# Second mixture of experts on chosen rows only: rows scattered into expert slots, 23 tiles of 512 slots, results scattered and added at the end

## The reference

```python
scores = softmax(xf @ Wg.T)                       # xf: 4096 rows of 128, normalised
expert_weights, expert_indices = top_k(scores, 2)
expert_weights = expert_weights / expert_weights.sum(-1)
gates = (one_hot(expert_indices, 8) * expert_weights[..., None]).sum(axis=1)
g = silu(lora_in(xf, W1, b1, A1, B1)) * lora_in(xf, W3, b3, A3, B3)   # all 8 experts, 256 wide
y_e = lora_out(g, W2, b2, A2, B2)
y = einsum('te,ted->td', gates, y_e)              # six of the eight gates of a row are zero
```

## Time and profile before

| what | value |
|---|---|
| median of 3 executions | 1125.36 us (1123.95 to 1134.6) |
| the profiled execution | 1127.59 us |
| its span, first to last instruction | 1126.4 us |
| TensorE, VectorE, ScalarE, GpSimd busy | 77%, 69%, 40%, 38% |
| second MoE in it | 799.2 to 1126.4 us |

### The profile page before, as it was taken

How to read it: one execution, slowest core, us unless ns; L and a number is a source line. 1 busy time by engine, 2 the same in 40 slices (tenths; PEclk the granted TensorE clock), 3 DMA queues, 4 the chain that set the end, 5 groups by cost and what they waited for, 6 DMA issues and landing times. The chain is left out here.

```text
span 1126.4 us, 20278 instructions
## 1 busy us (share of the span) xinstructions
PE 872.6 (77%) x6496; PEld 644.1 (57%) x6496; DVE 773.8 (69%) x3299; ACT 451.6 (40%) x1123; POOL 426.2 (38%) x767
## 2 busy tenths in 40 slices
PE   0976766765577998537891388988699999999998
PEld 0753433432374554424561256666488888888887
DVE  7949999999334886371130869999567666766664
ACT  1454445444103555101132657877333333333332
POOL 5213666666545542016663655655200100010000
PEclk9975666667557999767996569999799999999999
DMA  8211111111103000005533100000000000000000
GB/s 171 64 40 31 36 36 35 37 36 31 30 13 150 19 23 24 10 6 100 84 107 121 45 2 3 3 3 3 1 1 10 11 1 11 10 10 1 10 10 10
DMA packets 66078, 37.98 MB, mean 34 GB/s; under 512 B 39482, under 2 KB 60083, under 8 KB 65460
## 3 DMA queue, kind: packets, MB, share of 16 engines
q1 hardware_dynamic: 63206, 32.31, 10.5%
q0 software_dynamic: 2048, 4.20, 2.5%
q10 hardware_dynamic: 718, 0.17, 0.1%
HBM read 26.11 MB, written 10.55 MB: 33 GB/s over the span
## 5 line engine op out<-in xcount | busy, mean ns | idle before, releaser
L1759 ACT ACTIVATE e_sg<-e_ps,vec 128x512 f32<-128x512 f32 x128 | 88.1, 689 | 182.7 <-PE e_ps L1720 182.0
L1680 PEld LDWEIGHTS e_psy<-w_folded,e_hh 128*128 128x128 f32 x1024 | 124.1, 192 | 5.2
L1680 PE MATMUL e_psy<-w_folded,e_hh 128*128 128x128 f32 x1024 | 124.5, 275 | 0.0
L1858 DVE SCALAR_TENSOR_TENSOR e_hh<-e_ps,vec,e_sg 128x512 f32<-128x512 f32 x128 | 94.6, 748 | 42.5 <-ACT e_sg L1759 39.7
L1846 DVE SCALAR_TENSOR_TENSOR X<-e_psy,e_gs,X 128x128 f32<-128x128 f32 x256 | 72.1, 344 | 56.5 <-PE e_psy L1680 56.5
L1718 PE MATMUL e_ps<-e_XH,e_wh 128*128 128x512 f32 x256 | 110.0, 430 | 0.0
L1720 PE MATMUL e_ps<-e_XH,e_wl 128*128 128x512 f32 x256 | 101.7, 397 | 0.0
L1719 PE MATMUL e_ps<-e_XL,e_wh 128*128 128x512 f32 x256 | 101.4, 396 | 0.0
L1448 POOL TENSOR_SCALAR a_kb<-a_kr,a_m,a_bk 128x128 f32<-128x128 f32 x128 | 57.9, 452 | 51.8 <-issue 36.8
L758 DVE MATCH_REPLACE8 work<-m,work 128x64 f32<-128x64 f32 x384 | 75.8, 208 | 0.0
L745 DVE MAX8 m<-work 128x8 f32<-128x64 f32 x384 | 57.1, 210 | 0.0
(11 more groups left out here) (367 smaller groups left out, 2135.8 us busy)
## 6 DMA issues: line engine op xcount, KB each, us to landing
toe<-s4d_kernel SPq DMA_DIRECT2D x64, 64.0 KB
planes<-rt_zeros SPq DMA_DIRECT2D x4, 1024.0 KB, 6.9
ew<-in_L_ffn_ew SPq DMA_DIRECT2D x16, 256.0 KB
comb_y<-planes SPq DMA_DIRECT2D x16, 256.0 KB, 5.7
X<-in_x SPq DMA_DIRECT2D x4, 512.0 KB, 6.8
fold_wr<-in_L_ffn_W SPq DMA_DIRECT2D x16, 128.0 KB, 2.3
rows<-XT SPq DMA_DIRECT2D x8, 256.0 KB, 2.0
out_dram<-X SPq DMA_DIRECT2D x8, 256.0 KB, 2.3
```

What stands on the lines that cost most here:

```text
L1680: mm = pe.matmul(psy[j][:, k, :], hh[j][:, c, k * P:(k + 1) * P], G.w2[:, e, c, :], start=(c == 0 and k == 0), stop=(c == NC - 1), skip_gr ...
L1759: act.activation(sg[j][:, c, :], psh[0][c][:], ACT.Silu, bias=G.vec[:, k:k + 1]).then_inc(silu[c], 1)
L1858: dve.scalar_tensor_tensor(hh[j][:, c, :], psh[1][c][:], G.vec[:, k:k + 1], sg[j][:, c, :], ALU.add, ALU.mult).then_inc(hh_sb[c], 1)
```

## The change

`second_experts` is split in three phases, and two earlier phases prepare for it.

- `first_experts`: VectorE no longer makes `e_wh` and `e_wl`. SyncE's late DMAs get four more, which store the folded weights and biases of the eight experts in DRAM (`folded_weights`, 395 KB for each expert).
- `second_attention`: SyncE fills a DRAM table `expert_slots` with vacant rows by 79 DMAs of 128 x 2080 bytes (21 MB). A row of it has 130 words: 128 values, the number of the row's home, its gate.
- `second_router` (new): blocks b of 512 rows as before. VectorE picks the two experts of each row and computes each choice's slot from a running count; GpSimd stores the rows, 128 with each indirect DMA, 8 for each block. At the end VectorE writes a table of 23 tiles: which expert, and which first slot. 23 tiles of 512 slots suffice for any choice (8192 / 512 + 7). The biases of the output layer are added here.
- `second_experts` (new): a loop over the 23 tiles i. SyncE reads the tile's entry from the table, and loads its rows (`xr`, 4 buffers) and its expert's weights (`wf`, 3 buffers). TensorE turns the rows of tile i + 1, computes the hidden products of tile i and the output product of tile i - 1. The splitting into high and low parts is now done for each tile, for rows and weights. VectorE scales the results by the gate (`ys`, 3 buffers), and GpSimd scatters them to DRAM (`expert_pairs`) with 4 indirect DMAs for each tile.
- `combine_pairs` (new): both results of each row are loaded, VectorE adds them to `G.X`, and the output is stored.

The core of the diff (the old function is printed above):

```diff
+STILE = 512
+NTILE = 2 * B * T // STILE + NE - 1
+SROWS = (NE - 1) * B * T + NTILE * STILE
+SPARE = 2 * B * T
+ROW = D + 2
...
+                n13, n2 = 2 * HE, HE // P * D
+                kept = G.folded.rearrange("e p w -> p e w")
+                later += [(kept[:, :, 0:n13], G.w13[:].rearrange("d e m c p -> d e (m c p)")),
+                          (kept[:, :, n13:n13 + n2], G.w2[:].rearrange("p e c d -> p e (c d)"))]
+                for m, n in enumerate("13"):
+                    v = VEC["L1_ffn_b" + n][0]
+                    later += [(kept[:, :, n13 + n2 + 2 * m:n13 + n2 + 2 * m + 2], G.vec[:, v:v + 2 * NE].rearrange("p (e c) -> p e c", e=NE))]
...
-                    dve.tensor_copy(G.wh[:, e, :, :, :], G.w13[:, e, :, :, :]).then_inc(s["high"], 1)
-                    dve.wait_ge(s["high"], e + 1)
-                    dve.tensor_tensor(G.wl[:, e, :, :, :], G.w13[:, e, :, :, :], G.wh[:, e, :, :, :].bitcast(F32), ALU.subtract).then_inc(s["low"], 1)
...
+            @block.sync
+            def _(sp):
+                sp.wait_ge(s["vacant"], 1)
+                slots = G.slots.rearrange("(i p k) w -> p i k w", p=P, k=STILE // P)
+                n = SROWS // STILE
+                for i in range(n):
+                    sp.dma_start(slots[:, i, :, :], vacant[:]).then_inc(s["cleared"], 16)
+                sp.wait_ge(s["cleared"], n * 16)
...
+                dve.memset(vacant[:], 0.0).then_inc(s["spare"], 1)
+                dve.wait_ge(s["spare"], 2)
+                dve.tensor_copy(vacant[:, :, D:D + 1].bitcast(U32).rearrange("p k a -> p (k a)"), vacant_i[:]).then_inc(s["vacant"], 1)
...
-def second_experts(nc, C, A, G):
...
+def second_router(nc, C, A, G):
...
+                for b in range(NBLK):
+                    if b + 2 < NBLK:
+                        root(b + 2)
+                    pool.wait_ge(s["slot"], b + 1)
+                    pool.wait_ge(s["twice"], b + 1)
+                    for k in range(2):
+                        for t in range(TB):
+                            pool.indirect_dma_start(G.slots, bass.IndirectOffsetOnAxis(ap=slot[:, b, k, t:t + 1], axis=0),
+                                                    rb[b % NB][:, k, t, :], None).then_inc(sent[b % NB], 16)
+                for j in range(NB):
+                    pool.wait_ge(sent[j], 2 * TB * 16 * len(range(j, NBLK, NB)))
...
+                    after(dve, sent[b % NB], 2 * TB * 16 * (b // NB))
+                    normalise_block(dve, rb[b % NB][:, 0, :, 0:D], G.X[:, tiles(b), :], part(b)).then_inc(s["xs"], 1)
...
+                def choose(b):
+                    w = part(b)
+                    dve.wait_ge(s["logits"], b + 1)
+                    dve.tensor_copy(w["lg"], psl[:, 0:TB * NE].rearrange("p (k e) -> p k e", e=NE)).then_inc(s["lg"], 1)
+                    dve.wait_ge(s["lg"], b + 1)
+                    largest(b, 0)
+                    step.then(dve.scalar_tensor_tensor(w["lg"], oh[:, b, 0, :, :], TAKEN, w["lg"], ALU.mult, ALU.add))
+                    largest(b, 1)
+                    TT(w["d"], w["m1"], w["m0"], ALU.subtract).then_inc(s["d"], 1)
+                    step.then(TT(w["sel"], oh[:, b, 0, :, :], oh[:, b, 1, :, :], ALU.add))
+                    for t in range(b * TB, (b + 1) * TB):
+                        m = TT(run[:, t + 1, :], run[:, t, :], full["sel"][:, t, :], ALU.add)
+                        if t + 1 < (b + 1) * TB:
+                            step.then(m)
+                    m.then_inc(s["sel"], 1)
...
+                def place(b):
+                    w = part(b)
+                    dve.wait_ge(s["ranks"], b + 1)
+                    step.then(TT(w["pos"], psr[:, 0:TB * NE].rearrange("p (k e) -> p k e", e=NE), wide(first[:].unsqueeze(1), shape), ALU.add))
+                    step.then(TT(prod[:, b], oh[:, b], wide(w["pos"].unsqueeze(1), [P, 2, TB, NE]), ALU.mult))
+                    step.then(dve.tensor_reduce(slotf[:, b], prod[:, b], AX.X, ALU.add))
+                    dve.tensor_copy(slot[:, b], slotf[:, b]).then_inc(s["slot"], 1)
...
+                for b in range(NBLK):
+                    if b + 2 < NBLK:
+                        statistics(b + 2)
+                    choose(b)
+                    if b + 1 < NBLK:
+                        normalise(b + 1)
+                    gates(b)
+                    place(b)
+                    if b > 0:
+                        add_biases(b - 1)
+                table()
+def second_experts(nc, C, A, G):
...
+            @block.sync
+            def _(sp):
+                for i in range(NTILE):
+                    e = sp.value_load(G.tiles[0:1, 0, i:i + 1], min_val=0, max_val=NE - 1)
+                    row = sp.value_load(G.tiles[0:1, 1, i:i + 1], min_val=0, max_val=SROWS - STILE)
+                    if i >= NX:
+                        sp.wait_ge(kept[(i - NX) % NY], ((i - NX) // NY + 1) * S * 16)
+                    sp.dma_start(xr[i % NX][:], G.slots[bass.ds(row, STILE), :].rearrange("(p k) w -> p k w", k=S)).then_inc(rows[i % NX], 16)
+                    after(sp, s["y"], i - NW + 1)
+                    after(sp, hh_sb[NC - 1], i - NW + 1)
+                    sp.dma_start(wf[i % NW][:], G.folded[bass.ds(e, 1), :, :].rearrange("a p w -> p (a w)")).then_inc(weights[i % NW], 16)
+            @block.tensor
+            def _(pe):
+                def turn(i):
+                    pe.wait_ge(rows[i % NX], (i // NX + 1) * 16)
+                    after(pe, s["x_low"], i - 1)
+                    for k in range(S):
+                        mm = pe.transpose(pst[i % 2][:, k * P:(k + 1) * P], xr[i % NX][:, k, 0:D], G.ident[:])
+                    mm.then_inc(s["turned"], 1)
+                def product(i):
+                    j = i % 2
+                    after(pe, s["y_sb"], i - 1)
+                    for c in range(NC):
+                        pe.wait_ge(hh_sb[c], i + 1)
+                        for k in range(S):
+                            mm = pe.matmul(psy[j][:, k, :], hh[j][:, c, k * P:(k + 1) * P], wf[i % NW][:, 2 * HE + c * D:2 * HE + (c + 1) * D],
+                                           start=(c == 0 and k == 0), stop=(c == NC - 1), skip_group_check=True)
+                    mm.then_inc(s["y"], 1)
+                turn(0)
+                for i in range(NTILE):
+                    j = i % 2
+                    if i + 1 < NTILE:
+                        turn(i + 1)
+                    pe.wait_ge(s["x_low"], i + 1)
+                    pe.wait_ge(s["w_low"], i + 1)
+                    for c in range(NC):
+                        for m in range(2):
+                            after(pe, hh_sb[c], i)
+                            pe.matmul(psh[m][c][:], wh[j][:, m, c, :], XH[j][:], start=True, stop=False)
+                            pe.matmul(psh[m][c][:], wh[j][:, m, c, :], XL[j][:], start=False, stop=False)
+                            pe.matmul(psh[m][c][:], wl[j][:, m, c, :], XH[j][:], start=False, stop=True).then_inc(h_ps[m][c], 1)
+                    if i > 0:
+                        product(i - 1)
+                product(NTILE - 1)
+            @block.scalar
+            def _(act):
+                act.preload_act_table(ACT.Silu)
+                def high(i):
+                    act.wait_ge(weights[i % NW], (i // NW + 1) * 16)
+                    after(act, h_ps[1][NC - 1], i - 1)
+                    act.activation(wh[i % 2][:], w13(i), ACT.Copy).then_inc(s["w_high"], 1)
+                    act.wait_ge(s["turned"], i + 1)
+                    act.activation(XH[i % 2][:], pst[i % 2][:], ACT.Copy).then_inc(s["x_high"], 1)
+                high(0)
+                for i in range(NTILE):
+                    if i + 1 < NTILE:
+                        high(i + 1)
+                    for c in range(NC):
+                        k = 2 * HE + NC * D + c
+                        act.wait_ge(h_ps[0][c], i + 1)
+                        after(act, hh_sb[c], i - 1)
+                        act.activation(sg[i % 2][:, c, :], psh[0][c][:], ACT.Silu, bias=wf[i % NW][:, k:k + 1]).then_inc(silu[c], 1)
+            @block.gpsimd
+            def _(pool):
+                for i in range(NTILE):
+                    pool.wait_ge(s["y_sb"], i + 1)
+                    for k in range(S):
+                        pool.indirect_dma_start(G.pair, bass.IndirectOffsetOnAxis(ap=home[i % NY][:, k:k + 1], axis=0),
+                                                ys[i % NY][:, k, :], None).then_inc(kept[i % NY], 16)
+                for j in range(NY):
+                    pool.wait_ge(kept[j], S * 16 * len(range(j, NTILE, NY)))
+            @block.vector
+            def _(dve):
+                def low(i):
+                    dve.wait_ge(s["w_high"], i + 1)
+                    after(dve, h_ps[1][NC - 1], i - 1)
+                    dve.tensor_tensor(wl[i % 2][:], w13(i), wh[i % 2][:].bitcast(F32), ALU.subtract).then_inc(s["w_low"], 1)
+                    dve.wait_ge(s["x_high"], i + 1)
```

(70 more changed lines are left out.)

340 lines of the change are left out of this document (152 added, 188 removed).

## The result

The changed kernel takes 1159.06 us (median, 1155.36 to 1167.64), the kernel before 1125.09 on the same chip: a ratio of 1.0294 (95% interval 1.0214 to 1.0373). The profiled execution is the longest of them, 1167.64 us with a span of 1166.4. Of its excess 7.4 us lie in phases that the change leaves as they are: the phase that makes the first router's slots ends at 509.3 us here and at 501.9 in the trace of before. Some executions of most kernels are 7 to 14 us longer than their others, so where two versions are near each other I compare the phases in their traces.

A forecast was written before the change was run, and what follows sets the result against it. The prediction took TensorE alone to set the pace of the old second MoE. Start 799.2 + router 116 + tile loop 221.5 + adding the pairs 22 = 1158.7 us of span; forecast 1158 us, range 1132 to 1202.

The forecast's parts named there:

- Ahead of the phase, 0: Before the second MoE: vacant-row stores and folded weights cost 0 us, with ends of -3 and +5.
- The router, 116: Router phase: GpSimd's stores set it, one indirect DMA each 1.28 us; with start, inverse roots, landing and drain 116 us.
- VectorE is hidden: Router: VectorE needs 9.6 us for a block, less than GpSimd's 12, so it does not show.
- The weighed rule on VectorE shutting out GpSimd: Router: VectorE's float32 scalings keep GpSimd from writing descriptors, 9 us by the rule; left out of the sum.
- The tile loop, 221.5: Loop over 23 tiles: waiting for landed results sets the pace; with fill, last steps and drain 221.5 us.
- L: Tile loop: path from the end of an output product through scaling, stores and landing to the next rows, 11.1 us.
- T: Tile loop: length of a step, 9.0 us, half of a pair of 18.0 us; ends 8.05 and 11.5.
- the round trip does not bind: Rival, tile loop: GpSimd's stores set the pace, a step of 5.1 us, 1084 us in all; chance 0.06.
- The clock, 1.9 us a pair: Tile loop: after each pause TensorE starts at the lower level of 1.2 GHz, adding 1.9 us to a pair of steps.
- the clock stays low: Rival, tile loop: the clock stays at 1.2 GHz throughout, a step of 10.5 us, 1186 us in all; chance 0.17.
- The end of the loop: After the last product: GpSimd's remaining stores, landing, then a drain from 214.6 to 219.9 us, SyncE's first load at 221.5.
- the drains are shorter by half: Part of a rival: the clock holds (a step of 8.05 us) and both drains halve, 1134 us; chance 0.13.

The follow-up runs named there:

- the version with half the stores: Changed kernel with GpSimd storing only the first choices' rows in the router, 32 stores instead of 64; not a version to keep: 1138.72 us, ratio 1.0171.
- the three versions at 6.5: Changed kernel with rows loaded once VectorE has scaled tile i - 4 (0.9885); with five row buffers (0.9913); with that load rule plus four weight buffers (0.993).
- earlier release: Changed kernel, but SyncE loads the rows of tile i once VectorE has scaled tile i - 4, not once its results have landed: 1116.57 us, ratio 0.9885.
- work in the pause: Changed kernel with 22 matmuls on the identity, whose result nobody reads, ahead of every second tile's transposes: 1149.3 us, ratio 1.0201.

## Why the prediction was right

Against the profiled execution the four terms were:

| term | forecast | measured |
|---|---|---|
| start of the second MoE | 799.2 | 806.2 |
| router, to the first load of rows | 116 | 113.6 |
| tile loop, to the first load of results | 221.5 | 224.0 |
| adding the pairs, to the end | 22 | 22.5 |

The router came out 2.4 us shorter and the loop 2.5 us longer; that these cancel is luck, but either is small beside the 34 us of the slowdown.

*Ahead of the phase, 0.* This was right for the stores of vacant rows, which are all issued and waited for by 721.6 us, 84 us before the attention ends. The phase that stores the folded weights takes 106.3 us (509.4 to 615.7), before 106.1. The 7.0 us in the start are the 7.4 that this execution had lost before 509.3 us; the median, without them, is 1 us above the forecast.

*The router, 116.* The first store came at 15.0 us instead of 16, a block lasts 11.5 (821.19, 832.74, 844.27) where 8 x 1.28 + 1.7 are 11.9, the drain is 5.29. The step of the forecast that VectorE is hidden was right with little to spare: I had 9.6 us for its block, the version with half the stores shows 10 to 11. The weighed rule on VectorE shutting out GpSimd (the Trainium skill, SBUF — State Buffer, "SBUF: two separate sides") would have put 9 us on this phase by the prediction's estimate. The rows don't agree: 64 DMAs with 972 ns on average and 958 in the middle leave 0.9 us, and those beside a block's scalings (for example at 826.39 and 848.22) take 0.96 to 1.02.

*The tile loop, 221.5.* The steps were right one by one: L = 10.9 for 11.1, a pair 17.97 (the 18 steps from 946.76 to 1108.53 take 161.8) for 18.0, T = 8.99 for 9.0. The order of SyncE's queue made it so, and the versions with six row buffers show it from the other side: as soon as the circle is shorter than the steps that cover it, it costs nothing. The rival "the round trip does not bind" gave 1084 us for that; measured were 1073 to 1075, on chips where the kernel before takes 0.5% less than beside the changed one. Its condition, L of 5.2 us or less, holds only for four buffers. The general one is that with NX buffers TensorE does NX - 3 steps of 5 us between the product that fills a buffer and the transposes that want it again: 5 us for four buffers, 10 for five, 15 for six, against 10.9. This is worked out from the code; four and six are measured, and five give 6.0 us a step by it, with a slow start in each three steps, and 6.5 came out.

*The clock, 1.9 us a pair.* The pause does lead to a start at the 1.2 GHz level (0.78 us for the first hidden matmul, 0.47 when it follows work), and with the pause filled the first product of a pair ends 1.9 us sooner after its transposes. The term was right; that a pair got back only 1.6 of it has to do with the round trip, 0.3 us longer in that version. The rival that the clock stays low is out: 0.83 in the loop. The form is that of the Trainium skill's "HAM oscillation" (TensorE: Matmul & The Clock Gate): each wait for a DMA is followed by a start at half speed. Here too the trace agrees, by the 0.78 and 0.47 us.

*The end of the loop.* The one term that was mis-sized: I took the 5.3 us of drain from a phase with 64 indirect DMAs, and with 92 it is 7.56. That is 2.3 of the 2.5 us by which the loop is over. The rival in which the drains are shorter by half is out too.

What the forecast did not ask is what bounds the loop next, and there my expectations were wrong three times: 5.1 to 6.0 us a step, where 6.5 came out. Shown is that with six row buffers three weight buffers bind at 5.7 us, and that six and four together reach 5.0. What holds the three versions at 6.5 is not: in that with a fourth weight buffer the late signals are nearly as much as the excess, in the other two ScalarE waits longer for weights (77 and 81 us against 49), and all three ran on the one chip. A run of four or five row buffers with four weight buffers on another chip would tell.

Left open: why VectorE, with four row buffers, early release and four weight buffers, took its product some 3.5 us late in every second tile. It isn't the result buffers: those of three tiles back had landed long before, and ScalarE was kept waiting beside it. The wait is gone with six row buffers, but these ran on other chips, so I don't know whether the buffers or the chip took it away. Open as well is a wait in the router of the same kind: in four versions that leave the router's code alone (earlier release, five row buffers, four weight buffers, work in the pause) VectorE waits 8.9 to 12.4 us for logits ahead of the last block, though the matmuls had ended, and the phase takes 114.5 to 118.1 us instead of 110.1. These four are the ones that ran on the first chip of the experiments; on the others the same code takes 110.0 to 110.3 us. So the ratios of the first four are 4 to 8 us too high to be set beside later ones. The profile names nothing that ended the wait:

```profile
903.76 0.19 DVE L1794 COPY r_lg<-r_psl 128x32 f32<-128x32 f32 x1 [12.43 <-remote]
```

## What to carry to other kernels

When a buffer is given back only after its result has gone to DRAM and landed, lay out the whole circle (scale, issue, land, load) and count the steps that cover it: time per step times spare buffers must exceed it (needed, but not enough by itself: the weights have a circle of their own). Here two more buffers of rows and one of weights, two numbers in one line, turned a loss of 2.9% into a gain of 4.0%. A fourth weight buffer gave nothing beside four row buffers, in runs that another wait disturbed, and beside six it brought the step from 5.7 to 5.0 us. When a lifted limit gives less than its price, look in the trace for what ends the waits now, and raise its neighbours too before the idea is dropped. And run the versions that are to be compared on one chip. Computing a third of the work doesn't pay by itself: the router alone, which nothing covers any more, takes back 110 us of the 199 that TensorE's shorter work saves.

## What the runs showed of the hardware

- GpSimd's drain at the end of a phase grows with the indirect DMAs that the phase issued: 2.68 us after 32, 5.29 after 64, 7.56 after 92, the same within 1 ns in the versions read for it, and in the phase of before with 64. That is 82 to 84 ns for each. It runs although all of them have landed, and it costs at most 0.5 us when SyncE waits for the landings itself and goes on in the same block.
- GpSimd starts one indirect DMA of 128 rows each 1.26 us and is busy for 0.96 of it. The pace is the same in the router, and in the loop with six row buffers, where TensorE is never idle and DMA moves 185 GB/s.
- TensorE went through 80 us of the loop with six row buffers without a gap at a granted clock of 1.00, and the changed kernel, with 6 us of pause in each 18, got 0.83. Twenty-two small matmuls in each pause, of which nobody reads the result, brought 1.00 back.
- On one chip, in four versions, VectorE or ScalarE was released up to 12.4 us after the matmuls that it waited for had ended by the trace. On the other chips no such wait stands in the same phases. Its cause is open.
